# One product of 22 values per edge batch, and batch sums in two alternating pairs of PSUM banks, in a four-layer graph network kernel

## Time and profile before

| | |
|---|---|
| device time, 3 runs | 1400.4, 1402.16, 1404.18 us; median 1402.16 |
| span of the profiled execution, first to last instruction | 1400.5 us |
| busy share of the span | PE 97%, PEld 60%, DVE 63%, ACT 41%, POOL 6% |
| chain of work that ended last, by engine | PE 83%, DVE 11%, ACT 2%, issue 2%, DMA 1% |
| TensorE's mean granted clock | 0.991 of full speed |

### The profile page before, as it was taken

How to read it: one execution, slowest core, us unless ns; L and a number is a source line. 1 busy time by engine, 2 the same in 40 slices (tenths; PEclk the granted TensorE clock), 3 DMA queues, 4 the chain that set the end, 5 groups by cost and what they waited for, 6 DMA issues and landing times.

```text
span 1400.5 us, 26694 instructions
## 1 busy us (share of the span) xinstructions
PE 1363.9 (97%) x11285; PEld 843.1 (60%) x11285; DVE 886.7 (63%) x1381; ACT 568.6 (41%) x980; POOL 88.0 (6%) x86
## 2 busy tenths in 40 slices
PE   9889999989998999999999999999999999999998
PEld 8779898989996655544444444454444445344443
DVE  7998998999988886567555666542354223532323
ACT  2666566656554457411142113221253224422312
POOL 3120010101002110000001000011100000000000
PEclk9999999999999999999999999999999999999999
DMA  9634344335348723000002000022210222563201
GB/s 335 227 114 148 137 138 137 126 119 177 120 146 286 238 94 108 1 31 1 0 0 61 0 0 1 1 59 77 68 40 29 73 71 78 200 212 104 91 0 60
DMA packets 71333, 136.92 MB, mean 98 GB/s; under 512 B 11908, under 2 KB 24324, under 8 KB 69798
## 3 DMA queue, kind: packets, MB, share of 16 engines
q1 hardware_dynamic: 68542, 123.98, 26.8%
q0 software_dynamic: 1280, 5.77, 1.5%
q10 hardware_dynamic: 1384, 5.38, 1.1%
HBM read 81.79 MB, written 53.32 MB: 96 GB/s over the span
## 4 chain that ended last, share of the span: by engine, by line
PE 83%; DVE 11%; ACT 2%; issue 2%; DMA 1%; POOL 0%; ACTq 0%; SPq 0%; DVEq 0%; POOLq 0%
PE banks L2305 31%; PE banks L2239 13%; PE banks L2369 12%; PE banks L1255 6%; PE banks L1655 4%; DVE x_sb L894 3%; PE banks L1192 3%; PE banks L1209 2%; PE banks L1266 2%; PE banks L1166 2%; DVE x_sb L877 1%; PE banks L2183 1%; PE banks L1625 1%; PE banks L298 1%; PE banks L1643 1%
## 5 line engine op out<-in xcount | busy, mean ns | idle before, releaser
L2305 PE MATMUL banks<-g,count 128*128 128x512 f16 x1024 | 227.6, 379 | 0.5 <-DVE tiles L2571 0.5
L2305 PE MATMUL banks<-count,g 128*128 128x512 f16 x1024 | 223.6, 379 | 0.0
L2239 PE MATMUL banks<-w_parts,h_parts 128*128 128x512 f16 x960 | 215.3, 379 | 1.7 <-DVE g L2520 1.4
L2305 PEld LDWEIGHTS banks<-count,g 128*128 128x128 f16 x1024 | 99.6, 98 | 118.0
L2305 PEld LDWEIGHTS banks<-g,count 128*128 128x128 f16 x1024 | 99.7, 98 | 113.6 <-DVE tiles L2571 1.0
L2369 PE MATMUL banks<-g,part 128*128 128x512 f16 x768 | 165.9, 379 | 0.0
L2239 PEld LDWEIGHTS banks<-w_parts,h_parts 128*128 128x128 f16 x960 | 91.2, 98 | 115.4 <-issue 11.4
L894 DVE TENSOR_TENSOR x_sb<-eb_parts,x_sb 128x4096 f16<-128x4096 f16 x64 | 146.0, 2281 | 0.0
L1255 PE MATMUL banks<-x_sb 128*128 128x128 f16 x2048 | 126.9, 221 | 11.9 <-DVE x_sb L894 11.8
L1255 PEld LDWEIGHTS banks<-x_sb 128*128 128x128 f16 x2048 | 120.9, 99 | 15.3 <-DVE x_sb L894 14.2
L2369 PEld LDWEIGHTS banks<-g,part 128*128 128x128 f16 x768 | 75.1, 98 | 90.6
(11 more groups left out here) (346 smaller groups left out, 1902.5 us busy)
## 6 DMA issues: line engine op xcount, KB each, us to landing
weight_dram<-w_new SPq DMA_DIRECT2D x60, 256.0 KB, 2.6
count<-weight_dram SPq DMA_DIRECT2D x29, 512.0 KB, 7.1
qk_dram<-stage SPq DMA_DIRECT2D x64, 128.0 KB, 2.6
tiles<-x_dram SPq DMA_DIRECT2D x32, 256.0 KB, 3.5
x_dram<-tiles SPq DMA_DIRECT2D x32, 256.0 KB, 2.8
count<-in_x SPq DMA_DIRECT2D x4, 1024.0 KB, 12.8
h<-in_x SPq DMA_DIRECT2D x16, 256.0 KB, 4.3
h_dram<-h_t SPq DMA_DIRECT2D x8, 512.0 KB, 3.3
```

The costliest lines, as they stand in the source:

```text
L2239: mm = pe.matmul(out, m.h_parts[:, slot, zh, k], m.w_parts[:, zw, k], start=n == 0 and layer != 3, stop=n == len(passes) - 1)
L2305: mm = pe.matmul(m.agg_ps[:, b], lhs, rhs, start=i == 0 and z == 0, stop=i == NT - 1 and z == 1)
```

## The change

Three things change in the build; the results are the same sums.

1. **Marks and products of a batch.** Each unit and source tile now has a row of 24 float16 values (`VROW`) in `hot_val`: 16 bias parts (high, low), then two high weight parts, two low weight parts and two ones, one of each pair for each half of the partitions (the other half's is zero, set once by `mark_halves`), then the tile mark stored twice. DVE's batch is a comparison written straight into the last two values of each row, the source comparison, and one product of 22 values (`VALUES`) by the tile mark. The count comparison L872 and the product L887 are gone. `copy_part` and `residual` write the weights' parts separately for each half, 22 values apart. The 64-column matmul reads the high weights and the ones, the 32-column matmul the low weights, in pairs of values that lie 24 apart; the bias matmul reads 8 values out of 24.
2. **Sums.** A unit's sums take 64 columns rather than 128, so a batch fits two banks, and batches alternate between banks 3, 4 and 5, 6. PE's wait for ACT's copies is for batch n - 2 rather than n - 1. The in-degrees move to a slot of `work_ps`, and DVE reads them as soon as PE's batch is done. ACT reads the sums in the new order.
3. **Keys.** `prep_keys` reuses one of its integer rows, with one more wait; two POOL iotas go.

```diff
--- before.py
+++ after.py
-CW = 3 * CCOLS
 HP = 2 * H
+W_HI, W_LO, ONE = HP, HP + 2, HP + 4
+VALUES = HP + 6
+VROW = VALUES + 2
...
-    n_src, n_eb, n_cw, n_tile = (2 * BATCH * c for c in (P, NT * HP, CW, 2 * NT))
-    m.eb_parts = place("eb_parts", [P, 2, P, HP], F16, AT_EB)
+    n_src, n_val = (2 * BATCH * c for c in (P, NT * VROW))
+    m.parts = place("parts0", [P, P, VALUES], F16, AT_EB)[:], place("parts1", [P, P, VALUES], F16, AT_REST + 15360)[:]
...
+    m.hot_val = hots[:, n_src:n_src + n_val].rearrange("p (z g t c) -> p z g t c", z=2, g=BATCH, t=NT)
...
-    m.cw_ps = keep.banks[:, WORK:7].rearrange("p b (g c) -> p (b g) c", c=P)
-    m.deg_ps = m.cw_ps[0:2 * GTILES, 0:GROUPS, CW:P]
+    m.cw_ps = keep.banks[:, WORK:7].rearrange("p (z b) (g c) -> p z (b g) c", z=2, c=2 * CCOLS)
...
+        if i == 0:
+            use(("deg", t), ("added", t + 1 if first_round else n + 1))
...
-        dve.tensor_scalar(m.ints[:, 1], m.ints[:, 0], P - 1, None, ALU.bitwise_and)
-        dve.tensor_scalar(m.ints[:, 2], m.ints[:, 0], 7, None, ALU.logical_shift_right).then_inc(s["dve"], 1)
+        dve.tensor_scalar(m.ints[:, 1], m.ints[:, 0], P - 1, None, ALU.bitwise_and).then_inc(s["dve"], 1)
+        k += 1
+        dve.wait_ge(s["dve"], k)
+        dve.tensor_scalar(m.ints[:, 0], m.ints[:, 0], 7, None, ALU.logical_shift_right).then_inc(s["dve"], 1)
...
-        weight = m.fields[:, 2, units].unsqueeze(2).to_broadcast([P, units.stop - units.start, 2])
-        biases = m.fields[:, 3:FIELDS, units].rearrange("p h u -> p u h")
+        biases, parts = m.fields[:, 3:FIELDS, units].rearrange("p h u -> p u h"), m.parts[z]
         dve.wait_ge(s["copied"], part_count(t, piece, first_round))
-        dve.scalar_tensor_tensor(m.w_parts[:, z, units, 1], weight, keep.scale[:, 1:2], m.w_parts[:, z, units, 0], ALU.mult, ALU.subtract)
-        dve.scalar_tensor_tensor(m.eb_parts[:, z, units, H:HP], biases, keep.scale[:, 0:1], m.eb_parts[:, z, units, 0:H],
+        for half in range(2):
+            rows = slice(half * WHALF, (half + 1) * WHALF)
+            dve.scalar_tensor_tensor(parts[rows, units, W_LO + half], m.fields[rows, 2, units], keep.scale[rows, 1:2],
+                                     parts[rows, units, W_HI + half], ALU.mult, ALU.subtract)
+        dve.scalar_tensor_tensor(parts[:, units, H:HP], biases, keep.scale[:, 0:1], parts[:, units, 0:H],
                                  ALU.mult, ALU.subtract).then_inc(s["parts"], 1)
...
-        cw = m.hot_cw[:, z]
-
-        def key(which, c):
-            return m.keys[:, ts, which, units].unsqueeze(2).to_broadcast([P, BATCH, c // 2, 2])
+        hot = m.hot_val[:, z]
+        tile_hot = hot[:, :, :, VALUES:VROW]
         if n >= 2:
             dve.wait_ge(s["batch"], n - 1)
         if i == 0:
             dve.wait_ge(s["keyed"], t + 1)
-        dve.tensor_tensor(cw[:, :, 0:CCOLS].rearrange("p g (c two) -> p g c two", two=2),
-                          keep.iota_cnt[:].rearrange("p (c two) -> p c two", two=2).unsqueeze(1).to_broadcast([P, BATCH, NT, 2]),
-                          key(1, CCOLS), ALU.is_equal).then_inc(s["dve"], 1)
-        dve.tensor_tensor(m.hot_tile[:, z], keep.iota_tile[:].unsqueeze(1).to_broadcast([P, BATCH, NT, 2]),
-                          m.keys[:, ts, 1, units].unsqueeze(2).to_broadcast([P, BATCH, NT, 2]), ALU.is_equal).then_inc(s["dve"], 1)
+        dve.tensor_tensor(tile_hot, keep.iota_tile[:].unsqueeze(1).to_broadcast([P, BATCH, NT, 2]),
+                          m.tile_keys[ts][:, units].unsqueeze(2).to_broadcast([P, BATCH, NT, 2]), ALU.is_equal).then_inc(s["dve"], 1)
         dve.tensor_tensor(m.hot_src[:, z].rearrange("p g (c two) -> p g c two", two=2),
                           keep.iota_src[:].rearrange("p (c two) -> p c two", two=2).unsqueeze(1).to_broadcast([P, BATCH, P // 2, 2]),
-                          key(0, P), ALU.is_equal)
+                          m.src_keys[ts][:, units].unsqueeze(2).to_broadcast([P, BATCH, P // 2, 2]), ALU.is_equal)
         nonlocal k
-        k += 2
+        k += 1
         dve.wait_ge(s["dve"], k)
         if n == 0:
             residual(0)
         if units.start in [u.start for u in unit_parts(t, first_round)]:
             dve.wait_ge(s["parts"], part_count(t, 1 if units.start else 0, first_round))
-        dve.tensor_tensor(cw[:, :, CCOLS:CW].rearrange("p g (z c two) -> p g z c two", z=2, two=2),
-                          cw[:, :, 0:CCOLS].rearrange("p g (c two) -> p g c two", two=2).unsqueeze(2).to_broadcast([P, BATCH, 2, NT, 2]),
-                          m.w_parts[:, ts, units].unsqueeze(3).to_broadcast([P, BATCH, 2, NT, 2]), ALU.mult)
         for tile in turned:
             h_low(tile)
-        tiles = m.hot_tile[:, z].rearrange("p g t two -> p (g t) two").unsqueeze(2).to_broadcast([P, BATCH * NT, H, 2])
-        values = m.eb_parts[:, ts, units].unsqueeze(2).to_broadcast([P, BATCH, NT, HP])
-        dve.tensor_tensor(m.hot_eb[:, z].rearrange("p g (t c) -> p g t c", t=NT), values, tiles, ALU.mult).then_inc(s["hots"], 1)
+        tiles = tile_hot.rearrange("p g t two -> p (g t) two").unsqueeze(2).to_broadcast([P, BATCH * NT, VALUES // 2, 2])
+        values = m.parts[ts][:, units].unsqueeze(2).to_broadcast([P, BATCH, NT, VALUES])
+        dve.tensor_tensor(hot[:, :, :, 0:VALUES], values, tiles, ALU.mult).then_inc(s["hots"], 1)
+
+    def mark_halves():
+
+        for parts in m.parts:
+            settle(dve.memset(parts[:, :, HP:VALUES], 0.0))
+            for half in range(2):
+                dve.memset(parts[half * WHALF:(half + 1) * WHALF, :, ONE + half], 1.0)
+
+    def settle(op):
+        nonlocal k
+        op.then_inc(s["dve"], 1)
+        k += 1
+        dve.wait_ge(s["dve"], k)
...
-            dve.wait_ge(s["slab"], n + 1)
-            part = CPT // GROUPS
-            op = dve.tensor_tensor(keep.deg[:].rearrange("q b (g c) -> q b g c", c=part), m.deg_ps.rearrange("q g (c b) -> q b g c", c=part),
-                                   keep.deg[:].rearrange("q b (g c) -> q b g c", c=part), ALU.add)
+            bank, _ = uses["deg", n // NBATCH]
+            dve.wait_ge(s["batch"], n + 1)
+            op = dve.tensor_tensor(keep.deg[:], m.work_ps[0:2 * GTILES, bank, 0:P].rearrange("q (c b) -> q b c", c=CPT), keep.deg[:], ALU.add)
...
     pieces = projections(first_round)
+    mark_halves()
     if first_round:
         other_norms()
...
-        act.activation(m.w_parts[:, z, units, 0], weight, ACT.Copy, scale=keep.scale[:, 1:2])
-        act.activation(m.eb_parts[:, z, units, 0:H], biases, ACT.Copy, scale=keep.scale[:, 0:1]).then_inc(s["copied"], 1)
+        for half in range(2):
+            rows = slice(half * WHALF, (half + 1) * WHALF)
+            act.activation(parts[rows, units, W_HI + half], m.fields[rows, 2, units], ACT.Copy, scale=keep.scale[rows, 1:2])
+        act.activation(parts[:, units, 0:H], biases, ACT.Copy, scale=keep.scale[:, 0:1]).then_inc(s["copied"], 1)
...
-            act.copy(to_count, m.cw_ps[:, :, 0:CCOLS].rearrange("p (c b) (h s) -> p s c b h", c=GROUPS, h=2))
+            act.copy(to_count, sums[:, :, CCOLS:2 * CCOLS].rearrange("p (c b) (s h) -> p s c b h", c=GROUPS, h=2))
...
-        slab = m.w_slab[:, q % 2, n % 4].rearrange("p (b c) -> p b c", b=BATCH)
-        act.copy(slab, m.cw_ps[:, :, CCOLS:2 * CCOLS]).then_inc(s["slab"], 1)
+        slab = m.w_slab[:, q % 2, n % 4].rearrange("p (b h s) -> p b h s", h=2, s=NT)
+        act.copy(slab, sums[:, :, 0:CCOLS].rearrange("p b (s h) -> p b h s", h=2)).then_inc(s["slab"], 1)
...
-            parts = m.hot_eb[:, z, g].rearrange("p (t two h) -> p two t h", two=2, h=H)
+            parts = m.hot_val[:, z, g, :, 0:HP].rearrange("p t (two h) -> p two t h", two=2)
...
-        if n:
-            pe.wait_ge(s["slab"], n)
-            pe.wait_ge(s["added"], added(n - 1))
+        if n >= 2:
+            pe.wait_ge(s["slab"], n - 1)
+            if not first_round:
+                pe.wait_ge(s["added"], n - 1)
         if i == 0:
-            pe.matmul(m.deg_ps, keep.half_of[:, GTILES - 1 - t:3 * GTILES - 1 - t], keep.match[:], start=True, stop=True)
+            bank, free = uses["deg", t]
+            if free:
+                pe.wait_ge(s[free[0]], free[1])
+            pe.matmul(m.work_ps[0:2 * GTILES, bank, 0:P], keep.half_of[:, GTILES - 1 - t:3 * GTILES - 1 - t], keep.match[:], start=True, stop=True)
         for g in range(BATCH):
-            pe.matmul(m.cw_ps[:, g, 0:2 * CCOLS], m.hot_src[:, z, g], m.hot_cw[:, z, g, 0:2 * CCOLS], start=True, stop=False)
-            mm = pe.matmul(m.cw_ps[:, g, CCOLS:2 * CCOLS], m.hot_src[:, z, g], m.hot_cw[:, z, g, 2 * CCOLS:CW], start=False, stop=True)
+            hot = m.hot_val[:, z, g].rearrange("p t (c two) -> p c t two", two=2)
+            pe.matmul(m.cw_ps[:, z, g], m.hot_src[:, z, g], hot[:, W_HI // 2:ONE // 2 + 1:2], start=True, stop=False)
+            mm = pe.matmul(m.cw_ps[:, z, g, 0:CCOLS], m.hot_src[:, z, g], hot[:, W_LO // 2], start=False, stop=True)
```

(26 more changed lines are left out.)

6 lines of the change are left out of this document (1 added, 5 removed).

## The result

The changed kernel takes 1441.85 us (median of 4 runs, 1441.71 to 1443.38) against 1402.81 of the kernel before beside it (4 runs, 1400.40 to 1404.18): a ratio of 1.0288, 95% interval 1.0273 to 1.0303. It is slower, as forecast, but by 39 us and not by 7, and outside the range. The profiled execution took 1441.71 us, with a span of 1438.7. All of it lies in the build: from the end of the build (420.16 us before, 458.22 after) to the end of the span it is 980.3 and 980.5 us.

What follows compares the result with a forecast made beforehand. The prediction took PE and DVE, nearly in balance and changing places, to bound the build. Its terms, 0.6 + 1.6 + 2.2 + 0.6 + 1.9 = +6.9 us, added to the runs' median of 1402.2, gave 1409 us; range 1399 to 1424.

Steps and rivals of the forecast that it cites:

- At nothing: Parts charged 0 us: PE's matmuls reading pairs, ACT's copies of the sums, the in-degrees' new slot and earlier reading, POOL iotas.
- the second rival: TensorE reads pairs more slowly: +0.08 us a batch, 1412 us, or +0.45 a batch, 1428 us; chance 14%.
- Marks and products: DVE's comparisons and product: a batch goes from 4.62 to 4.65 us, +0.6 us on 19 chain batches (-2.7 to +17).
- the third rival, dear words: DVE's hopping single-word writes in the tile comparison cost 5.1 ns each, +0.90 us a batch: 1426 us and up; chance 7%.
- Residuals: DVE's weight remainders become two hopping instructions on 64 partitions: +0.36 us each, six times, +2.2 us (0 to +6.2).
- The late features: Two batches where DVE waits for ACT's features: the whole product now lies behind the wait, 3.00 instead of 2.20 us, +1.6 us.
- Keys: One DVE instruction of `prep_keys` now stands behind a wait: 0.1 us, six times on the chain, +0.6 us (0 to +0.9).
- Marking the halves: Six memsets and two waits ahead of the first keys, 2.2 us on DVE: +1.9 us (0.5 to 2.5).
- The banks: Alternating banks for the sums and the in-degrees' new slot: PE never felt the relaxed wait, DVE's lead is lost; 0 us.
- The last rival: Faster: free words and DVE's lead from the 6.5 us of in-degree waits lasting into its next stretch: 1395 us; chance 13%.
- three signs: Forecast wrong if PE's pairs are further apart, the product leaves 0.52 ns a value, or PE's 11.8 us of waits shrink.
- The wait ahead of the in-degrees: DVE's wait for ACT before adding in-degrees, 6.5 us before: expected nearly gone, with more waits for PE in its place.

Runs made afterwards that it cites:

- e2: The changed kernel with only the moving operands of the two sum matmuls read contiguously (sums not the reference's): 1421.31 us, ratio 1.0145.
- e1: The kernel before with only the moving operands of the two sum matmuls read in pairs of values 48 bytes apart: 1426.29 us, ratio 1.0180.
- e8: The kernel before with both sum matmuls reading runs of two values that begin 16 bytes apart: 1426.25 us, one run.
- e9: The kernel before with only the first, 64-column sum matmul reading runs of two values 48 bytes apart: 1420.64 us, one run.
- e6: The kernel before with both sum matmuls reading runs of four values 48 bytes apart: 1402.14 us, one run.
- e7: The kernel before with both sum matmuls reading runs of two values that begin 8 bytes apart: 1402.01 us, one run.
- e10: e4 with the weights' parts made as before, by broad instructions on all 128 partitions and a product with a mask of the halves: 1407.99 us, ratio 1.0046.
- e3: The kernel before with only the alternating banks, the in-degrees' new slot and the later waits; marks and products as before: 1402.19 us, ratio 1.0000.
- e4: The changed kernel with each row turned, pairs of values outermost, so matmuls read runs of 32 or more: 1418.67 us, ratio 1.0118.
- e11: e10 with the ones written by two copies of a mask behind the first keys, in place of the six memsets: 1407.22 us, ratio 1.0044.
- e12: e11 with DVE making a batch's product ahead of the low part of the features, not behind it: 1404.68 us, ratio 1.0019.

## Why the prediction was wrong

*The step that failed* is the one under "At nothing": "L1255 already reads runs of 8 values ... I take the same for reads of 2 values, since L1255 is nearest in engine and operand". It was nearest in all but what counts: its runs of 8 values fill 16 bytes, a pair fills 4. PE's 0 should have been +0.56 us a batch, which alone is 20 to 24 us (e2, e1). The mechanism was in the text as the second rival, at 14%, and even its upper price, 0.45 us a batch, was too low. The Trainium skill (Advanced Engine Details and Errata, SBUF Cachelines) speaks of two hits on a line of 16 bytes; here two values a piece cost a 64-column matmul as much again as it takes (e8, e9), and four cost nothing (e6, e7). The measurement decides, and by it I should not have let the page weigh against that rival.

*Marks and products* held. The product takes 3.00 us from start to start. The comparison takes 0.44 to the next one's start where 0.51 was forecast:

```profile
152.80 0.61 DVE L873 TENSOR_TENSOR x_sb<-iota_tile,tile_key 128x512 f16<-128x512 f16 x1
153.24 1.23 DVE L875 TENSOR_TENSOR x_sb<-iota_src,src_key 128x2048 f16<-128x2048 f16 x1
```

The chain puts 0.53 on it, but then only 1.05 on the comparison behind it (1.14 before), so a batch on DVE is 0.53 + 1.05 + 3.00 = 4.58, forecast 4.65. The hop of a word costs (0.44 - 0.34) / 256 = 0.4 ns (0.70 forecast), so the third rival, dear words, falls; the Trainium skill's figure (Vector Engine (DVE) Microarchitecture Reference, Measured stream behaviour on trn2) had given an estimated 0.71 us, which is too much for this output.

*Residuals* were right in kind and too small: 1.50 us in place of 0.40, +1.1, where +0.36 was charged; that is beyond the upper bound of +1.04. The two instructions hop on both sides, as L2526 does, and that row was the right neighbour, not the one that hops on its output alone. *ACT's copies* of the weights are in no term of the sum: two of 0.87 us stand for one of 0.52, and where the chain runs through ACT the stretch takes 3.74 us in place of 2.39, +1.35, twice. The 10.7 us that e10 gave back are both together, with the clock that goes with them, after its mask product has taken some 2.2 us (0.36 on six tiles) of the gain.

*The late features*: putting the product ahead of the wait gave back 2.5 us, so +1.6 was the right kind of term; that the wait itself grew, from 5.0 us in two places to 11.7 in four, no term had. *Keys*: from the product to the next comparison 1.53 to 1.74 us at four places of the chain, in place of 1.40: +0.13 to +0.34 where +0.1 was charged. *Marking the halves*: 3.6 us for a forecast of 2.2, and the first keys at 54.64 us, not 52.4; that it delays the first batch is seen, what of it reaches the end is open. *The banks*, at nothing: right, by e3.

The last rival, that DVE's lead is kept and the kernel gets faster, fell as argued: in e3 the lead goes straight into the wait for PE. Of the three signs that I named of a wrong forecast, two came: pairs that start further apart, and PE's 11.8 us of waits, which shrank to 9.6 as TensorE became the slower of the two. The wait ahead of the in-degrees, which should have nearly gone, was 4.8 us, now for PE.

From the changed kernel down, in one line: 1441.9, less 23.2 for the turned row, which are the reads above all (e4), less 10.7 for the parts of the weights (e10), less 0.8 for the ones (e11), less 2.5 for the order (e12), is 1404.7.

## What to carry to other kernels

A layout that lets one DVE instruction write for several readers is paid for by each reader: look at how many neighbouring values each of them finds in 16 bytes, TensorE's moving operand too, and order the values by TensorE's reads where the writer doesn't mind (the turned product, with the parts read pair by pair, took the same 3.00 us). When a cost isn't in the trace, a row on the same engine is no neighbour if its runs are longer: here no row had reads in pairs by a matmul, and a small run of its own (as e1) would have given the price. And where two engines are in balance, a stall of TensorE can be followed by a lower clock for the batch behind it, so that a price worked out from durations alone can be too low.
